# Unread products of constants on TensorE in two stretches of a graph layer with attention and experts

## The reference

```python
xn = layernorm(x)                                   # 1250 x 512
# messages: for each edge (src = where it arrives, dst = where it reads)
h   = softplus(edge_attr_20 @ Wf1 + bf1) - log 2    # 40000 x 128, hidden of the edge
W   = (h @ Wf2 + bf2) * edge_weight                 # filters of the edge
msg = products of the gathered node row (xn @ W_in), direction of the edge and W
agg = segment_sum(msg, src)                         # 1250 nodes
gnn = W2 applied to (softplus of, or as it is) agg @ W1
# attention over all nodes, linear: q, k = elu + 1
mix = layernorm(xn + (q (k^T v) / norm) @ Wo) * gamma + beta
x   = x + gnn + mix
# experts: 8 of width 1024, the best 2 for every node
y_e = (silu(z @ w_gate[e]) * (z @ w_up[e])) @ w_down[e],  z = layernorm(x)
return x + sum over the two experts of weight * y_e
```

## Time and profile before

| what | value |
| --- | --- |
| median of three runs | 1508.92 us (1506.2 to 1512.41) |
| the profiled execution | 1510.84 us |
| its span, first to last instruction | 1509.1 us |
| TensorE busy | 1358.9 us, 90% |
| VectorE busy | 992.7 us, 66% |
| POOL busy | 743.0 us, 49% |
| ScalarE busy | 627.3 us, 42% |
| mean clock granted to TensorE | 0.951 of full speed |

### The profile page before, as it was taken

The page is one execution under the profiler, slowest core; times in us unless marked ns, Lnnn a source line. Parts: engine busy times, 40 slices in busy tenths (PEclk is TensorE's granted clock), DMA queues, the critical chain, the costliest instruction groups (busy, mean ns, idle before and its releaser), DMA issues.

```text
span 1509.1 us, 24446 instructions
## 1 busy us (share of the span) xinstructions
PE 1358.9 (90%) x6707; PEld 642.4 (43%) x6708; DVE 992.7 (66%) x2486; ACT 627.3 (42%) x1097; POOL 743.0 (49%) x767
## 2 busy tenths in 40 slices
PE   6476998877869999999999999874999999999997
PEld 4243444444534444444444444462433333433333
DVE  7845666567737777777777777775655565556554
ACT  5454555545525666666666666471011101111110
POOL 4777777777766555556656555204312211211121
PEclk9768999989979999999999999996999999999999
DMA  5665333333249888888888888582342551524513
GB/s 200 223 215 164 114 116 117 112 112 112 98 143 292 251 247 248 248 249 250 250 239 259 250 248 249 157 307 69 71 146 77 188 188 28 195 64 147 193 28 94
DMA packets 125874, 262.50 MB, mean 174 GB/s; under 512 B 21073, under 2 KB 64808, under 8 KB 125147
## 3 DMA queue, kind: packets, MB, share of 16 engines
q0 software_dynamic: 48416, 141.37, 31.4%
q1 hardware_dynamic: 77410, 120.57, 23.9%
HBM read 204.35 MB, written 63.66 MB: 178 GB/s over the span
## 4 chain that ended last, share of the span: by engine, by line
PE 61%; POOL 22%; issue 8%; DMA 4%; DVE 3%; SPq 1%; ACT 0%; POOLq 0%; DVEq 0%; ACTq 0%
POOL edge_list L456 20%; PE psum L1368 20%; PE psum L1856 17%; PE psum L1868 8%; PE psum L1381 7%; PE psum L1376 5%; PE psum L1363 2%; DMA xrow<-in_x 1%; POOL slot_list L1788 1%; SPq L374 1%; DMA out_x<-out_sums 1%; PE psum L1863 1%; DMA slot_list<-pair,slots 1%; PE psum L1474 0%; PE psum L1559 0%
## 5 line engine op out<-in xcount | busy, mean ns | idle before, releaser
L1259 POOL DMA_INDIRECT shared<-node_table,shared x328 | 310.9, 948 | 211.5 <-DVE msg L1336 127.3
L456 POOL DMA_INDIRECT edge_list<-rec,place x313 | 316.7, 1012 | 97.0 <-issue 95.2
L1338 DVE TENSOR_TENSOR msg<-shared,psum 128x768 f32<-128x768 f32 x328 | 309.7, 944 | 0.0
L1368 PE MATMUL psum<-wf,hT 128*128 128x512 f32 x656 | 305.4, 608 | 2.8 <-ACT psum L1293 2.2
L1856 PE MATMUL psum<-shared,zT 128*64 128x512 f32 (+1 forms) x960 | 295.6, 597 | 1.9 <-DVE zT L1974 1.6
L1293 ACT COPY psum<-bias 128x512 f32<-128x512 f32 x328 | 193.3, 590 | 210.8 <-DVE msg L1338 194.1
L1336 DVE TENSOR_TENSOR msg<-shared,psum 128x256 f32<-128x256 f32 x328 | 135.6, 413 | 138.3 <-PE psum L1368 121.5
L1856 PEld LDWEIGHTS psum<-shared,zT 128*64 128x64 f32 (+1 forms) x960 | 114.4, 159 | 180.8 <-issue 178.6
L1368 PEld LDWEIGHTS psum<-wf,hT 128*128 128x128 f32 x656 | 118.3, 190 | 155.1 <-issue 138.0
L1868 PE MATMUL psum<-shared,hidT 128*64 128x512 f32 (+1 forms) x480 | 152.7, 596 | 3.5 <-DVE hidT L1995 3.5
L1816 POOL DMA_DIRECT2D ids<-slot_list x20 | 11.7, 585 | 290.5 <-DVE zN L1943 266.4
(11 more groups left out here) (351 smaller groups left out, 1510.5 us busy)
## 6 DMA issues: line engine op xcount, KB each, us to landing
shared<-edge_list SPq DMA_DIRECT2D x332, 130.0 KB
shared<-in_L_ffn_w_gate SPq DMA_DIRECT2D x8, 2048.0 KB, 9.0
shared<-in_L_ffn_w_up SPq DMA_DIRECT2D x8, 2048.0 KB, 14.7
shared<-in_L_ffn_w_down SPq DMA_DIRECT2D x8, 2048.0 KB, 19.5
shared<-node_table,shared POOLq DMA_INDIRECT x328
edge_list<-rec,place POOLq DMA_INDIRECT x313, 2.6
raw<-in_records SPq DMA_DIRECT2D x19, 256.0 KB, 3.2
xrow<-in_x SPq DMA_DIRECT2D x10, 250.0 KB
```

Source lines behind the costliest of these rows:

```text
L456: nc.gpsimd.indirect_dma_start(out=edge_list, out_offset=bass.IndirectOffsetOnAxis(ap=place[:n_, c:c + 1].bitcast(U32), axis=0), in_=rec[: ...
L1259: nc.gpsimd.indirect_dma_start(out=gat[:, k % G, :], out_offset=None, in_=table, in_offset=bass.IndirectOffsetOnAxis(ap=ix, axis=0)).then_ ...
L1338: nc.vector.tensor_tensor(m[:, 1:7, :].rearrange("p (a i) f -> p a i f", a=2), g[:, P:D].rearrange("p (i f) -> p i f", i=3).unsqueeze(1).t ...
L1368: nc.tensor.matmul(WP[k % TS][:], hT[:, (k // TS) % 2, (k % TS) * P:(k % TS + 1) * P], wf2[:], start=False, stop=True, skip_group_check=Tr ...
```

## The change

Three edits.

1. At the start of the messages TensorE waits until the records of the last but one group have been placed, and then multiplies the identity by 512 columns of constants four times, into the second turning bank. Nobody reads the result; the bank is overwritten by the second `turn_hidden`.
2. At the start of the experts it does six such products ahead of the first `first_tokens` and three behind the second, into the first gate bank, which block 0 overwrites.
3. The semaphore `count_column` is merged into the one of the radial weights (`wf1_clear`, now "opening_memsets"). POOL's memsets all count that one up, and the thresholds of those that wait move along: 1 becomes 2 for the radial weights, the column's 1, 2 and 3 become 1, 3 and 4.

```diff
-            column_s, PAIRED = sem("count_column"), NB // 2
+            PAIRED = NB // 2
...
-                "inputs_cleared", "radial_weights_cleared", "ones_column", "edges_turned", "edges_copied",
+                "inputs_cleared", "opening_memsets", "ones_column", "edges_turned", "edges_copied",
...
-                    sp.wait_ge(wf1_clear, 1)
+                    sp.wait_ge(wf1_clear, 2)
...
-                    nc.gpsimd.memset(ks[:, 0, 0:D // 2], 0.0).then_inc(column_s, 1)
+                    nc.gpsimd.memset(ks[:, 0, 0:D // 2], 0.0).then_inc(wf1_clear, 1)
                     nc.gpsimd.memset(half[:], 0.5)
                     nc.gpsimd.memset(wf1[:], 0.0).then_inc(wf1_clear, 1)
-                    nc.gpsimd.memset(col_b[:], 0.0).then_inc(column_s, 1)
-                    pool.wait_ge(column_s, 2)
-                    nc.gpsimd.memset(col_b[:, NB - 1:NB + P // 2:P // 2], 1.0).then_inc(column_s, 1)
+                    nc.gpsimd.memset(col_b[:], 0.0).then_inc(wf1_clear, 1)
+                    pool.wait_ge(wf1_clear, 3)
+                    nc.gpsimd.memset(col_b[:, NB - 1:NB + P // 2:P // 2], 1.0).then_inc(wf1_clear, 1)
...
-                    pe.wait_ge(column_s, 1)
+                    pe.wait_ge(wf1_clear, 1)
...
-                    pe.wait_ge(column_s, 3)
+                    pe.wait_ge(wf1_clear, 4)
...
-                            act.wait_ge(wf1_clear, 1)
+                            act.wait_ge(wf1_clear, 2)
...
-                    act.wait_ge(wf1_clear, 1)
+                    act.wait_ge(wf1_clear, 2)
...
+                IDLE_EDGES = 4
...
                         ins.then_inc(opened, 1)
+                        pe.wait_ge(placed[(NQ - 2) % 3], 16 * QC * len(range((NQ - 2) % 3, NQ - 1, 3)))
+                        for k in range(IDLE_EDGES):
+                            nc.tensor.matmul(TP[1][:], ident, const[:, 0:4 * P], start=True, stop=True)
                         turn_hidden(0, 0, 16 * TS)
...
+                    def idle_products(n_):
+                        for k in range(n_):
+                            nc.tensor.matmul(GATE[0][:], ident, const[:, 0:4 * P], start=True, stop=True)
+
+                    idle_products(6)
                     first_tokens(0)
                     first_tokens(1)
+                    idle_products(3)
                     pe.wait_ge(routed, STARTS)
```

## The result

The changed kernel took 1513.81 us (median of 11 runs, 1511.45 to 1520.28) beside 1509.35 us for the kernel before on the same chip (11 runs, 1504.4 to 1513.08). The ratio is 1.0033, 95% interval 1.0020 to 1.0046: some 4.5 us slower. The forecast was 1508.6 us, in a range from 1505.2 to 1512.6; the time lies above it.

The account below looks back on a forecast made before the run. TensorE was 61% of the chain, but POOL's late target list bounds block 1. Only 0.34 us at the messages counted, all else 0: 1508.92 us less 0.34 gives 1508.6 us, range 1505.2 to 1512.6.

Parts of the forecast that it names:

- the semaphore: Merging the count column's semaphore into the radial weights' one releases nothing earlier or later: 0.
- the cover of the six products: Experts' start: six products end at 1035.2 or 1036.3, hidden before the picks at 1036.78, 0.5 to 1.5 us to spare.
- The cover of the four products: Messages' start: the products end at 443.6, leaving 1.9 us before the first turning at 445.52.
- The three products: Behind the token products, taken at half clock: turning starts 2.3 us late, yet block 0 gains 0.8 us overall.
- 0, as long as the clock stays up over the longer wait: Block 1: block 0's gain of 0.8 to 3.1 us is given back waiting for hidT, so nothing counts.
- rival 1: Longer wait ahead of block 1's down products drops the clock: 2.1 us slower than forecast, 1510.7 us; 25%.
- From there TensorE is dense ... and so keeps it: Messages: TensorE restarts 0.34 us before 455.12, when the filter banks are refilled, and keeps that to the edges' end.
- The sign that the prediction gave for itself: Prediction is wrong if the end of the messages' first supertile moves by more than 0.5 us.
- The term of 0.34 us: Messages: the second message no longer waits for a filter, so 0.34 us is gained.
- rival 4: Messages: the clock falls again before 445.52, or the second message waits for something else: 0, 1508.9 us; 8%.
- Rival 3: Experts: the six products overrun to 1038.9 and slot entries come 2.2 us late: 1510.8 us; 8%.
- Rival 2: Block 0's gain is kept if the target list comes sooner or block 1's wait is short: 1505.8 us; 12%.

Follow-up runs that it names:

- six_only: The changed kernel with only the six products ahead of the token picks and the merged semaphore, no products at the messages; 0.9997 of before (0.9986 to 1.0008).
- before_look1: A second profiled execution of the unchanged kernel before; wait for the filter banks 2.39 us, wait for hidT 2.88 us, six down records 2.84 us.
- late_gate: The kernel before, no unread products; in block 1 alone VectorE scales block 0's rows behind the second half's product, not first; 0.9972 of before, 1505.29 us.
- edges_filled: The changed kernel with only the messages' four products, plus two more between the second turning and the fourth filter; 1.0005 of before (0.9990 to 1.0019).

## Why the prediction was wrong

- *What held:* the semaphore (no cost that six_only shows), the cover of the six products, and what goes to full speed. The six took 7.67 us (6.7 to 7.8 forecast; 8.13 and 6.50 in the two further executions) and ended before the picks in all three; the four took 3.60 us (3.47); block 0 gained what was said. The wait in block 1 grew from 3.50 to 6.12 us, in the range of 4.3 to 6.6.
- *The cover of the four products,* 1.9 us, was not there. It was read from a wait of 5.50 us for the first records; in before_look1 that wait is 2.56 us. The turning started 7.25, 6.25 and 7.26 us after the last record issue in the three executions of the changed kernel, 6.38 to 6.40 before: in two of them later than its records landed, which the prediction names as a refutation of this part. That this cost nothing in the end is luck: the gathers, not the turning, led to the messages.
- *The three products:* the turning starts 4.42 us after the start of the last token products (1039.07 to 1043.49), 3.31 before: 1.1 us later and not 2.3, so block 1's wait came near the upper end of its range and not the lower one that I took.
- *The step that failed at the experts* is "0, as long as the clock stays up over the longer wait". It did not stay up: in all five traces with the three products, the early scaling and no added delay, the six down records took 4.43 to 5.45 us in place of 2.84, a loss of 1.6 to 2.6 us. This is rival 1 with its place and its price of 2.1 us; its weight was wrong, and so was the reading by which before's runs hold such falls already and the change adds part of one. I kept it down to 25% because the spread of before's runs might already hold such falls. Of six traces with a slow block 0 and the old order in block 1, one did.
- *The step that failed at the messages* is "From there TensorE is dense ... and so keeps it". I read the wait for the filter banks only as the place from which the gain is kept, and not as a wait that the faster filters lengthen: counted from POOL's last record issue TensorE came to it 1.2 us sooner (at 12.7 and not 13.8 us) and left it no sooner (16.1 and 16.0 us). The same mechanism as rival 1, at a second place, was no rival at all. The sign that the prediction gave for itself, an end of the first supertile moved by more than 0.5 us, came with it (23.32 beside 21.50 us). Four of the five traces with the four products and no fill fell there, one of nine without products.
- *The term of 0.34 us* is not shown. The wait for the filter banks ended 16.12, 16.15 and 15.48 us after the last record issue in the changed kernel, 16.00, 15.94 and 15.65 before, and the second message, once free of the filter, started no sooner. In that, *rival 4* was right ("or the second message waits for something else, 0"); what held the message for its last 0.20 us the profile does not name. Rival 4's time, 1508.9, was not measured.
- *Rival 3* (the six overrun) did not come about. *Rival 2* (the gain is kept) needed block 1's wait gone; with late_gate it is gone, and the traces, not the times, show the gain.
- *The range* ended at 1512.6 since one fall was in it. With a second, at the messages' price of 4.52 - 2.84 = 1.7 us, the slow end is 1508.6 + 2.1 + 1.7 = 1512.4, and from before's median in these rounds, 0.4 us higher, 1512.8: past the range even without scatter.

## What to carry to other kernels

In this kernel, work that only raised TensorE's clock ahead of a wait that another engine ended moved idle time from in front of the work to behind it, and the clock then fell there, where TensorE ended last. So look at the next wait after every stretch that becomes faster, ask how long it will be, and price a fall for each. Here it was better to ask why the engine waits at all: moving one VectorE instruction off the head of block 1 brought 0.28%, the products at their best nothing that could be measured.

## What the runs showed of the hardware that was not expected

More work made a kernel faster: five further unread products in front of block 0 took it from 1.0026 to 1.0001 of before, 3.8 us, give or take 2.8. And the length of a wait alone does not say whether the clock falls: 3.50 us in block 1 held it, 3.47 us at the same place, in edges_filled, did not.
